# Joint rotation of two tiles, groups of three inner chunks, and an earlier start of the placing in a vision block with routed experts

## The chip, the cores and the metric

One core of a Trainium2 chip runs the whole program. The metric is device microseconds from launch to end; three runs of the kernel before were made, and one further execution was profiled. Times in the text are microseconds from the start of the span. The engines are called PE (TensorE), DVE (VectorE), ACT (ScalarE), POOL (GpSimd) and SP (SyncE, which only issues transfers).

## The reference

64 images of 224 x 224 become 196 patches each, 12544 rows of width 192 in all, and pass one block of a vision tower:

```
h = patches @ W + b
q, k, v = heads(layernorm(h))            # 12 heads of 16, q and k rotated by position
w = erf(q k^T / 4) + 1, causal; h = h + (w v / sum w) @ Wproj.T
x = layernorm(h)
probs = softmax(x @ Wr)                  # 8 experts, the best two per row, shares normed
each expert takes the 3920 rows that gave it the largest shares
expert(x) = (silu(x @ w1) * (x @ w3)) @ w2      # inner width 768
out = h + sum of chosen experts * share + shared expert(x)
```

All is float32. The rows chosen by an expert are scattered back with addition.

## The kernel before

**Attention** works in turns, one unit of two images (392 rows, four tiles) a turn, 32 units; turns overlap three stages, so that a turn computes the patch products of a later unit, norms and products q, k, v of the next one, the weights of its own, and the projection of the previous one. Each turn has twelve steps `n`, one per pair of heads. The order on every engine is written out by hand, as `if n == ...` lines. On DVE a step is multiply_x (L549), weigh (L556), a reciprocal (L608) and floor (L564), with other work between: at n == 3 and n == 4 the rotation of q and k, two tiles each (L626 to L633), at n == 5 the addition of the projection (L653), at n == 11 the bias (L663). The rotation takes the copy `qk_raw` that ACT made (L411 called from L445), multiplies it by a table of cosines and by one of sines, tile by tile (four instructions over 384 elements), waits, and forms differences and sums (four over 192). `settle` is a wait for all `step`s before. On ACT, at n == 3: a copy of scores (L420), the gelu (L435), two copies of the turned normed rows (`LN1T`, L439), then other copies. On PE, at n == 3: scores, weighted sums, the transposes of the normed rows (L734), twelve products of the second token tile (L748), which need the bank of the first `LN1T` copy, then q and k (L741), v, the turned outputs and at n == 5 the projection (L741 from L798). POOL multiplies the weights (L690) between ACT's gelu and DVE's weigh. Turn `u` is followed by the next without a gap.

**Routing.** `choices` forms for every row the two best experts and their shares, and then searches each expert's threshold, two bits a step (`search_and_place`, steps s = 0 to 15, s = 16 settles). Steps 0 to 10 run alone; the others, and the placing steps, run between chunks of the first five shared units, one step behind each pair of chunks (`behind_pair`, L1316). After the last count POOL sends the level to memory and back, spread over the experts (L1453, L1456). Step 17 is empty. Steps 18 to 23 rank the rows: two scans, each with a count on PE (`add_counts`, L1057), then `slots_of` for the first choices (s = 22) and for the second (s = 23), each of which raises `placed`. POOL waits for both, then scatters 196 entries into the table with indirect transfers (L1464), first and second choice of a row group in turn, never more than two in flight.

**Shared and expert units.** 25 shared units (512 rows, the last 256: SHORT) and 64 expert units (8 per expert, 490 rows) have one form. The inner width 768 is six chunks `m`. All products are in float16 parts, high and low. For a pair of chunks PE computes gate and up, per chunk eight whole-height matmuls (L1245 to L1248) and then, for both chunks, a half-height matmul for gate and one for up which run side by side (L1251, L1253). Behind each pair it issues a third of the output matmuls of the unit before (72 in all, L1274 to L1276). ACT forms the silu (L1290) and the high half of the hidden values (L1284), DVE the product (L1309) and the low half (L1302). Gate and up have two PSUM banks each; PE waits at a chunk until the chunk two before has been multiplied:

```
for m in (2 * pair, 2 * pair + 1):
    pe.wait_ge(T.multiplied, MI * g + m + 1)
```

The rows for an expert unit come by POOL's gather (L1476, four transfers by ids), are split into halves by ACT (L1576, L1577) and DVE (L1661, L1663), inside the unit before, behind chunk m == 1 (`split_at`; 3 in a whole shared unit), and SP issues four transposing transfers (L1428). Results are scaled by ACT (`put`, L1593) and scattered by POOL (L1487). Ahead of the first expert ACT and DVE split its weights behind the last whole shared unit (L1195, L1211).

## Time and profile before

| | |
|---|---|
| three runs | 3376.86, 3378.2, 3385.53 us, median 3378.2 |
| the profiled execution | 3376.83 us, span 3374.7 us |
| mean granted clock of PE | 0.945 of full speed |
| busy, share of the span | PE 3091.8 us (92%), DVE 2446.8 (73%), ACT 1526.7 (45%), POOL 1377.0 (41%) |
| instructions of the rotation | L626 and L627 x128 each over 384 elements, L631 and L633 x128 each over 192 |
| chunk work, mean of one | DVE L1309 670 ns, L1302 667 ns; ACT L1290 582 ns, L1284 601 ns |

Attention fills the span up to about 1600 us, the routing that runs alone up to about 1720, the shared units up to about 2200, and the experts the rest. In the timeline views a row has the start and the time taken of a merged run of like instructions; a number in brackets is the idle time of the engine ahead of it, with what ended it. The time between the starts of two instructions can be shorter than the first one takes.

### The profile page before, as it was taken

To read this page: it belongs to the slowest core of one execution; us is meant where nothing else is said; L and a number is where in the kernel's file an instruction comes from. 1 tells how busy PE (TensorE), PEld (TensorE's weight loads), DVE (VectorE), ACT (ScalarE), POOL (GpSimd) and SP (SyncE) were. 2 spreads that over 40 slices of the span, in tenths; PEclk is the share of its full clock that TensorE was granted. 3 is DMA by queue.
4 is the path that set the end of the run, shared out by engine and by line. 5 is a ranking of instruction groups with operands and counts; after the bars stand their busy time and mean duration, and the time that the engine had idled before them with its cause. 6 is when DMAs were issued, how large, how long until landed. Compare 5 with 4: busy or idle time off the path is not lost. (4 is left out here: it accounts for less than half of the span.)

```text
span 3374.7 us, 70939 instructions
## 1 busy us (share of the span) xinstructions
PE 3091.8 (92%) x25828; PEld 2110.6 (63%) x25828; DVE 2446.8 (73%) x4893; ACT 1526.7 (45%) x3223; POOL 1377.0 (41%) x1172
## 2 busy tenths in 40 slices
PE   6999999999999999998059999899999999999997
PEld 5777777777777777766025555556666556566664
DVE  6999999999999999997766555554555455455543
ACT  2444444444444444443024444444555455455443
POOL 1332233223332332322202555536666555655664
PEclk9899999999999999986579999999999999999999
DMA  3333333323332333322122222245554555545442
GB/s 104 77 75 78 73 87 80 81 66 87 89 76 68 81 89 75 75 46 54 45 67 67 74 67 78 59 95 101 77 96 71 98 71 97 101 69 97 77 75 42
DMA packets 460505, 260.36 MB, mean 77 GB/s; under 512 B 337967, under 2 KB 441759, under 8 KB 456063
## 3 DMA queue, kind: packets, MB, share of 16 engines
q1 hardware_dynamic: 392448, 196.41, 24.3%
q0 software_dynamic: 54464, 49.01, 10.3%
q10 hardware_dynamic: 13262, 10.66, 0.9%
q8 instruction: 192, 3.15, 0.4%
q14 instruction: 139, 1.14, 0.1%
HBM read 107.98 MB, written 68.15 MB: 52 GB/s over the span
## 5 line engine op out<-in xcount | busy, mean ns | idle before, releaser
L1309 DVE SCALAR_TENSOR_TENSOR ffn_hidden<-ffn_up,ffn_silu 128x490 f32<-128x490 f32 (+2 forms) x534 | 350.6, 670 | 676.2 <-ACT ffn_silu L1290 510.9
L690 POOL TENSOR_TENSOR weights<-weights,x_pair 128x400 f32<-128x400 f32 x384 | 396.3, 1032 | 828.7 <-DVE weights L556 810.1
L1290 ACT ACTIVATE ffn_silu<-ffn_gate 128x490 f32<-128x490 f32 (+2 forms) x534 | 301.9, 582 | 735.6 <-PE ffn_up L1253 541.6
L1487 POOL DMA_INDIRECT out_rows<-done,ids x256 | 407.4, 1591 | 407.6 <-ACT done L1593 346.4
L608 DVE RECIPROCAL recip<-x_product 128x200 f32<-128x200 f32 x384 | 534.2, 1391 | 0.0
L1274 PE MATMUL ffn_out<-ffn_w_hi,ffn_hidden_hi 128*128 128x192 f16 (+1 forms) x2124 | 525.6, 247 | 3.9 <-DVE ffn_hidden_lo L1302 2.0
L1275 PE MATMUL ffn_out<-ffn_w_lo,ffn_hidden_hi 128*128 128x192 f16 (+1 forms) x2124 | 522.8, 246 | 0.0
L1276 PE MATMUL ffn_out<-ffn_w_hi,ffn_hidden_lo 128*128 128x192 f16 (+1 forms) x2124 | 522.7, 246 | 0.0
L748 PE MATMUL bank<-w_tok,patches 128*128 128x192 f32 x1536 | 327.2, 370 | 56.8 <-ACT normed_t L411 32.7
L1302 DVE TENSOR_TENSOR ffn_hidden_lo<-ffn_hidden,ffn_hidden_hi 128x490 f16<-128x490 f32 (+2 forms) x534 | 356.3, 667 | 15.9
L1284 ACT CAST ffn_hidden_hi<-ffn_hidden 128x490 f16<-128x490 f32 (+2 forms) x534 | 320.7, 601 | 91.9 <-DVE ffn_hidden L1309 90.7
L748 PEld LDWEIGHTS bank<-w_tok,patches 128*128 128x128 f32 x1536 | 290.4, 217 | 72.8 <-ACT normed_t L411 39.2
L1476 POOL DMA_INDIRECT tokens<-dram_x,ids x256 | 279.1, 1090 | 91.1 <-issue 76.2
L420 ACT ACTIVATE x_pair<-score 128x400 f32<-128x400 f32 x384 | 192.5, 502 | 269.2 <-DVE weights L556 180.4
L857 PE MATMUL y_sum<-v_held,weights 128*64 128x68 f32 (+1 forms) x1536 | 262.4, 253 | 31.5 <-DVE weights L564 31.5
L1274 PEld LDWEIGHTS ffn_out<-ffn_w_hi,ffn_hidden_hi 128*128 128x128 f16 (+1 forms) x2124 | 219.2, 103 | 110.3 <-issue 98.5
L1464 POOL DMA_INDIRECT dram_table<-entry,slot_of x196 | 202.9, 1035 | 207.4 <-issue 131.8
L435 ACT ACTIVATE weights<-x_pair 128x400 f32<-128x400 f32 x384 | 205.0, 534 | 182.0 <-PE y_sum L863 177.5
L741 PE MATMUL bank<-w_qkv,normed_t 96*128 96x192 f32 (+1 forms) x1024 | 275.5, 418 | 0.7 <-ACT normed_t L411 0.7
L859 PE MATMUL y_sum<-v,weights 128*64 128x51 f32 (+2 forms) x1536 | 248.3, 244 | 0.0
L1245 PE MATMUL ffn_gate<-ffn_tokens,ffn_w_hi 128*128 128x490 f16 (+2 forms) x534 | 199.8, 374 | 36.3 <-DVE ffn_tokens L1230 12.4
L741 PEld LDWEIGHTS bank<-w_qkv,normed_t 96*128 96x128 f32 x1024 | 180.3, 192 | 68.9 <-issue 4.4
(176 smaller groups left out, 6862.2 us busy)
## 6 DMA issues: line engine op xcount, KB each, us to landing
patches<-in_patches SPq DMA_DIRECT2D x32, 1176.0 KB, 5.2
ffn_raw<-in_w SPq DMA_DIRECT2D x18, 768.0 KB
dram_x_t<-x_t SPq DMA_DIRECT2D x32, 392.0 KB, 3.7
x_t<-dram_x_t SPq DMA_DIRECT2D x24, 512.0 KB
base<-dram_h SPq DMA_DIRECT2D x24, 384.0 KB, 4.2
out_rows<-sums ACTq DMA_DIRECT2D x24, 384.0 KB, 4.6
v_held<-v SPq DMA_DIRECT2D x64, 102.0 KB, 2.3
dram_h<-h SPq DMA_DIRECT2D x32, 192.0 KB
```

Of the source, the lines that this page charges most:

```text
L608: nc.vector.reciprocal(recip[:, n % 2], x_product[:, n % 2]).then_inc(inverted, 1)
L690: nc.gpsimd.tensor_tensor(weights[:, n % 4], weights[:, n % 4], x_pair[:, n % 4, ::-1], ALU.mult)\
L741: last = nc.tensor.matmul(out, wide(lhs, k, t), rhs[:, k, 0:width], start=(k == 0), stop=(k == 1))
L748: last = nc.tensor.matmul(out, wide(patches[slot], i, n), tok_w[:, i, :], start=(i == 0), stop=(i == KP - 1))
L1274: nc.tensor.matmul(out, hi, w_hi[:, m, :], start=(m == 0), stop=False)
L1275: nc.tensor.matmul(out, hi, w_lo[:, m, :], start=False, stop=False)
L1276: last = nc.tensor.matmul(out, lo, w_hi[:, m, :], start=False, stop=(m == MI - 1))
L1284: nc.scalar.copy(T.hidden_hi[slot][:, m, 0:n], T.hidden[:, m % 2, 0:n]).then_inc(T.hi_ready, 1)
L1290: nc.scalar.activation(T.silu[:, m % 2, 0:n], T.gate[m % 2][:, 0:n], ACT.Silu, scale=1.0 / (TOKEN_SCALE * WEIGHT_SCALE)).then_inc(T.silued, 1)
L1302: nc.vector.tensor_tensor(T.hidden_lo[slot][:, m, 0:n], T.hidden[:, m % 2, 0:n], T.hidden_hi[slot][:, m, 0:n], ALU.subtract).then_inc(T.lo ...
L1309: nc.vector.scalar_tensor_tensor(T.hidden[:, m % 2, 0:n], T.up[m % 2][:, 0:n], HIDDEN_SCALE / (TOKEN_SCALE * WEIGHT_SCALE), T.silu[:, m % ...
L1487: nc.gpsimd.indirect_dma_start(out=dram["out"][:, :], out_offset=bass.IndirectOffsetOnAxis(ap=ids[i][0:height, t, 0:1], axis=0), in_=done[ ...
```

## The change

Four things change. In the attention the rotation handles two tiles in one instruction: two multiplications over 768 elements and two sums over 384 in place of four and four, after a wait for both tiles' copies; and ACT's two `LN1T` copies stand ahead of the gelu at n == 3. In the routing the placing steps begin at 17 rather than 18, and POOL scatters all first choices as soon as they have their slots, then all second choices. In the shared units from the sixth on and in all expert units chunks go in groups of three: three banks for gate and up (the third are the routing's two banks `total` and `offset`), a wait at a chunk for the one three before, the half-height matmuls of three chunks together, and half of the unit before's output matmuls behind each group; ACT and DVE index the banks by `m % group`. Between the fifth and the sixth shared unit PE waits for all multiplications. The split of the next rows stands ahead of the chunks in expert units, behind the last chunk in the SHORT unit, and behind chunk 2 in the others of groups of three. The last output part is issued as one.

```diff
-        by_cos = [sb(f"by_cos{s}", [128, 2 * NH, 2, HD // 2]) for s in range(2)]
-        by_sin = [sb(f"by_sin{s}", [128, 2 * NH, 2, HD // 2]) for s in range(2)]
+        by_cos = sb("by_cos", [128, 2, 2 * NH, 2, HD // 2])
+        by_sin = sb("by_sin", [128, 2, 2 * NH, 2, HD // 2])
...
+                    if n == 3 and has_next:
+                        for k, pos in enumerate(LN1T):
+                            copy_out(pos, normed_t[:, k * UT:(k + 1) * UT], KD)
...
-                    if n == 3 and has_next:
-                        for k, pos in enumerate(LN1T):
-                            copy_out(pos, normed_t[:, k * UT:(k + 1) * UT], KD)
...
                         for i in range(2):
-                            t = 2 * (n - 3) + i
-                            dve.wait_ge(free[QK[t] % NB], fills(kind, u, QK[t]))
-                            src = qk_raw[:, t, :].rearrange("p (h c f) -> p h c f", h=2 * NH, c=2)
-                            if i == 0:
-                                settle()
-                            step(nc.vector.tensor_tensor(by_cos[i][:], src, over(tables[:, i, 0, :], shape), ALU.mult))
-                            step(nc.vector.tensor_tensor(by_sin[i][:], src, over(tables[:, i, 1, :], shape), ALU.mult))
+                            dve.wait_ge(free[QK[t + i] % NB], fills(kind, u, QK[t + i]))
                         settle()
-                        for i in range(2):
-                            t = 2 * (n - 3) + i
-                            step(nc.vector.tensor_tensor(rotated[:, t, :, 0:HD // 2], by_cos[i][:, :, 0, :],
-                                                         by_sin[i][:, :, 1, :], ALU.subtract))
-                            step(nc.vector.tensor_tensor(rotated[:, t, :, HD // 2:HD], by_cos[i][:, :, 1, :],
-                                                         by_sin[i][:, :, 0, :], ALU.add))
+                        src = qk_raw[:, t:t + 2, :].rearrange("p i (g f) -> p i g f", f=HD // 2)
+                        for c, out in enumerate((by_cos, by_sin)):
+                            table = tables[:, :, c, :].unsqueeze(2).to_broadcast([128, 2, 4 * NH, HD // 2])
+                            step(nc.vector.tensor_tensor(out[:].rearrange("p i h c f -> p i (h c) f"), src, table, ALU.mult))
+                        settle()
+                        step(nc.vector.tensor_tensor(rotated[:, t:t + 2, :, 0:HD // 2], by_cos[:, :, :, 0, :],
+                                                     by_sin[:, :, :, 1, :], ALU.subtract))
+                        step(nc.vector.tensor_tensor(rotated[:, t:t + 2, :, HD // 2:HD], by_cos[:, :, :, 1, :],
+                                                     by_sin[:, :, :, 0, :], ALU.add))
...
-PLACING = SEARCHED + 2
+PLACING = SEARCHED + 1
...
+    T.gate.append(R.total)
+    T.up.append(R.offset)
...
+def units_group(g):
+    return 2 if isinstance(g, int) and g < ROUTING else 3
...
+def tensor_group(nc, pe, T, g, slot, ws, n, part, group):
+    chunks = range(group * part, group * part + group)
...
+        pe.wait_ge(T.multiplied, MI * g + m + 3 - group)
...
+def tensor_out(nc, pe, T, g, slot, ws, tiles, part, parts):
...
-    share = len(tiles) * MI // 3
-    for k in range(third * share, (third + 1) * share):
+    share = len(tiles) * MI // parts
+    for k in range(part * share, (part + 1) * share):
...
 def scalar_unit(nc, act, T, g, slot, n, split, split_at):
+    if split_at is None:
+        split()
...
-            pool.wait_ge(R.placed, 2)
-            pool.sem_inc(spacer, 1)
-            for n in range(2 * PER):
+            for n, (c, t) in enumerate((c, t) for c in range(2) for t in range(PER)):
+                at = 2 * t + c
+                if t == 0:
+                    pool.wait_ge(R.placed, c + 1)
+                    pool.sem_inc(spacer, 1)
                 if n >= 2:
 
                     pool.wait_ge(dispatched[n % 2], 16 * (n // 2))
                     pool.sem_inc(spacer, 1)
                 nc.gpsimd.indirect_dma_start(
                     out=dram["table"][:, :],
-                    out_offset=bass.IndirectOffsetOnAxis(ap=slot_of[:, n:n + 1], axis=0),
-                    in_=entry[:, 2 * n:2 * n + 2], in_offset=None, bounds_check=SLOTS - 1, oob_is_err=False)\
+                    out_offset=bass.IndirectOffsetOnAxis(ap=slot_of[:, at:at + 1], axis=0),
+                    in_=entry[:, 2 * at:2 * at + 2], in_offset=None, bounds_check=SLOTS - 1, oob_is_err=False)\
...
+                group = units_group(g)
+                for part in range(MI // group):
+                    tensor_group(nc, pe, T, g, slot, 0, columns_of(tiles), part, group)
                     if isinstance(g, int) and g < ROUTING:
                         add_counts(nc, pe, R, SERIAL + 3 * g + part)
                     if not (isinstance(g, int) and g == 0):
-                        tensor_out(nc, pe, T, g - 1, 1 - slot, 0, WHOLE, part)
+                        tensor_out(nc, pe, T, g - 1, 1 - slot, 0, WHOLE, part, MI // group)
+                if isinstance(g, int) and g == ROUTING - 1:
+                    pe.wait_ge(T.multiplied, MI * g + MI + 2)
+                    pe.wait_ge(R.placed, 2)
...
+                for part in range(2):
+                    tensor_group(nc, pe, T, g, 1 - i % 2, ws, XU, part, 3)
                     if opening(e, i):
-                        tensor_out(nc, pe, T, g - 1, 0, 0, SHORT, part)
+                        tensor_out(nc, pe, T, g - 1, 0, 0, SHORT, part, 2)
                     else:
-                        tensor_out(nc, pe, T, g - 1, i % 2, 1 - ws if i == 0 else ws, ROUTED, part)
+                        tensor_out(nc, pe, T, g - 1, i % 2, 1 - ws if i == 0 else ws, ROUTED, part, 2)
...
-            for part in range(3):
-                tensor_out(nc, pe, T, SHARED + XUNITS - 1, 0, 0, ROUTED, part)
+            tensor_out(nc, pe, T, SHARED + XUNITS - 1, 0, 0, ROUTED, 0, 1)
...
-                scalar_unit(nc, act, T, g, slot, columns_of(tiles), split_next, 1 if tiles is SHORT else 3)
+                scalar_unit(nc, act, T, g, slot, columns_of(tiles), split_next, MI - 1 if tiles is SHORT else 2 if units_group(g) == 3 else 3)
...
-                scalar_unit(nc, act, T, g, 1 - i % 2, XU, split_next, 1)
+                scalar_unit(nc, act, T, g, 1 - i % 2, XU, split_next, None)
...
```

DVE's `vector_unit` is changed as `scalar_unit` is.

## Rows read from the trace of the kernel before

**Rows 1.** Busy time by stretch; after the span PE, PEld, DVE, ACT, POOL, clock, DMA

```profile
917.16:964.27 47.11, 45.28 (x440) 35.07 (x440) 45.94 (x104) 22.83 (x53) 14.45 (x14) 0.96 0.31 80
964.27:1012.73 48.46, 45.32 (x440) 35.10 (x440) 46.19 (x104) 22.59 (x53) 14.46 (x14) 0.96 0.34 78
...
2210.00:3340.00 1130.00, 1122.20 (x8316) 676.84 (x8314) 577.55 (x921) 569.73 (x1153) 660.96 (x492) 1.00 0.49 85
```

**Rows 2.** DVE in order of time, the rotation at n == 3, turn A

```profile
931.62 0.55 DVE L626 TENSOR_TENSOR by_cos<-qk_raw,rope 128x384 f32<-128x384 f32 x1
932.09 0.55 DVE L627 TENSOR_TENSOR by_sin<-qk_raw,rope 128x384 f32<-128x384 f32 x1
...
933.61 0.36 DVE L631 TENSOR_TENSOR rotated<-by_cos,by_sin 128x192 f32<-128x192 f32 x1
933.89 0.35 DVE L633 TENSOR_TENSOR rotated<-by_cos,by_sin 128x192 f32<-128x192 f32 x1
...
935.00 0.37 DVE L549 SCALAR_TENSOR_TENSOR x_product<-x_pair 128x200 f32<-128x200 f32 x1 [0.23 <-DVE rotated L633]
```

**Rows 3.** ACT in order of time, n == 3, turn A

```profile
924.47 0.50 ACT L420 ACTIVATE x_pair<-score 128x400 f32<-128x400 f32 x1 [1.82 <-DVE weights L556]
924.87 0.53 ACT L435 ACTIVATE weights<-x_pair 128x400 f32<-128x400 f32 x1
925.30 0.85 ACT L411 COPY normed_t<-bank 96x392 f32<-96x392 f32 x2
```

**Rows 4.** PE in order of time, the same place in turns A and B

```profile
925.82 2.22 PE L748 MATMUL bank<-w_tok,patches 128*128 128x192 f32 x12 [1.17 <-ACT normed_t L411]
...
972.93 3.64 PE L748 MATMUL bank<-w_tok,patches 128*128 128x192 f32 x12 [1.25 <-ACT normed_t L411]
```

**Rows 5.** DVE in order of time, addition of the projection in turn B

```profile
990.81 0.56 DVE L653 TENSOR_TENSOR h<-bank,h 128x384 f32<-128x384 f32 x1 [0.46 <-PE bank L741]
992.01 0.56 DVE L653 TENSOR_TENSOR h<-bank,h 128x384 f32<-128x384 f32 x1 [0.64 <-PE bank L741]
```

**Rows 6.** PE in order of time, one pair of chunks in an expert unit

```profile
3102.88 0.37 PE L1245 MATMUL ffn_gate<-ffn_tokens,ffn_w_hi 128*128 128x490 f16 x1
...
3105.98 0.37 PE L1248 MATMUL ffn_up<-ffn_tokens,ffn_w_hi 128*128 128x490 f16 x1
3106.29 0.38 PE L1251 MATMUL ffn_gate<-ffn_tokens,ffn_w_lo 64*128 64x490 f16 x1
...
3106.81 0.26 PE L1274 MATMUL ffn_out<-ffn_w_hi,ffn_hidden_hi 128*128 128x192 f16 x1
...
3108.80 0.37 PE L1245 MATMUL ffn_gate<-ffn_tokens,ffn_w_hi 128*128 128x490 f16 x1
```

**Rows 7.** POOL in order of time, levels and first table scatter

```profile
1769.09 0.96 POOL L1456 DMA_DIRECT2D levels<-dram_level  x1 [4.28 <-DMA dram_level<-level]
1816.00 1.07 POOL L1464 DMA_INDIRECT dram_table<-entry,slot_of  x1 [45.95 <-issue]
```

**Rows 8.** The tile levels, how long its transfer took

```profile
DMA to landing us min/median/max: 5.0/5.0/5.0
```

**Rows 9.** DVE in order of time, the first placing step

```profile
1778.73 0.98 DVE L923 TENSOR_TENSOR scratch<-key,levels 128x784 f32<-128x784 f32 x1
...
1780.75 1.79 DVE L1076 TENSOR_TENSOR_SCAN running<-carry,key 128x784 f32<-128x784 f32 x1
```

**Rows 10.** PE in order of time, the count behind the first scan

```profile
1782.60 0.39 PE L1057 MATMUL offset<-running,before 128*128 128x8 f32 x2 [3.05 <-DVE running L1076]
```

**Rows 11.** PE in order of time, the short unit ahead of the experts

```profile
2182.88 0.39 PE L1245 MATMUL ffn_gate<-ffn_tokens,ffn_w_hi 128*128 128x256 f16 x1 [7.88 <-DVE ffn_hidden L1309]
...
2193.75 0.28 PE L1245 MATMUL ffn_gate<-ffn_tokens,ffn_w_hi 128*128 128x256 f16 x1 [4.36 <-issue]
```

**Rows 12.** ACT in order of time, the start of an expert unit

```profile
3080.34 1.35 ACT L1593 ACTIVATE done<-ffn_out,ids 128x192 f32<-128x192 f32 x4
```

**Rows 13.** POOL in order of time, the last gather for that unit

```profile
3077.03 1.00 POOL L1476 DMA_INDIRECT tokens<-dram_x,ids  x1 [0.30 <-issue]
```

39 lines of the change are left out of this document (19 added, 20 removed).

## The prediction

> **What bounds the kernel now.** I read the page's slices first: VectorE (DVE) is at nine tenths or more through the attention, nothing is full in the middle where the routing is worked out, and TensorE (PE) is full from the shared units to the end. Then busy time by stretch, in which the reader should see two things [rows 1]. Two neighbouring turns of the attention loop (one turn is one unit of two images), which I call A and B, last 47.11 and 48.46 us, with DVE busy for 45.94 and 46.19 us of them; and over 1130 us of experts PE is busy for 1122.20 us at full clock. The busy figure is short of the truth for DVE: instructions start before the one in front has ended (931.62, then 932.09, each 0.55 us long [rows 2]). So in turn A DVE is the bound. The 31 turns alternate between these two kinds in most of the stage.
>
> In order of time, B differs from A at one place. The 12 products of the second token tile take 2.22 us in A and 3.64 us in B, both behind a wait for ACT's copy of the turned normed rows, of 1.17 and 1.25 us [rows 4]. 3.64 us is what the half clock (1.2 GHz) makes of it for most of its length; the mean granted clock is 0.96 in both turns [rows 1], so A has such a drop too, elsewhere, where PE has time. All PE work from there to the projection is one string, so in B the projection is 1.42 us late, and DVE waits for it, 0.46 and 0.64 us [rows 5]. With the overlap lost at either wait (some 0.08 us each) that is nearly the whole 1.35 us by which B is longer. So B is bound by PE from that copy to the projection, A by DVE with next to nothing to spare (1.42 less 1.26: about 0.1 us).
>
> **Part 1, the joint rotation.** A multiplication over 384 elements starts 0.47 us ahead of the next, a sum over 192 elements 0.28 us [rows 2]. 192 elements more cost 0.19 to 0.20 us, so the fixed part is 0.07 to 0.09 us, and I take 0.07. The block from 931.62 to 935.00 is 3.38 us long; four of its eight instructions fall away and the elements stay: 4 x 0.07 = 0.27 us, or 0.54 us for the two blocks of a turn. New is a wait: the first multiplication needs both tiles copied. Queued behind it are the rotation and everything on DVE after it, and POOL, which waits for DVE's next weighting. In A both copies are in before DVE comes. In B the second multiplication pair of the first tile hides the second copy now; some 0.5 us of wait can appear there, but it takes its time from the wait at the projection, which comes later in the same turn, so I price it at nothing. As for the duration of an instruction rather than its distance: the Trainium skill (VectorE: DVE Perf Modes, "The TRN2 errata") puts a float32 tensor_tensor at (N+151)/0.96 ns, thus 0.157 us fixed. The trace's 0.55 us durations agree with it, its distances don't; by that fixed part the turn would lose 1.26 us rather than 0.54.
>
> **Part 2, the copies ahead of the gelu.** ACT runs the score copy at 924.47, the gelu at 924.87 and both copies from 925.30 [rows 3]. The copies move ahead of the gelu: 925.30 - 924.87 = 0.43 us earlier, and so does PE's string. The gelu comes 0.85 us later; POOL needs it only one DVE iteration of over 3 us after that, so this costs nothing. The PE transposes that the copies need are done before the score copy is.
>
> **What both make of a turn.** A: 47.11 - 0.54 = 46.57 us, for the projection comes 0.43 us earlier and there was 0.1 us of room. B: the saved DVE time only lengthens the wait; what counts is PE's 0.43 us, or half of it (0.21) where the half clock stays where it is in time, since then 0.43 us more of the products fall under it. So 48.46 becomes 48.03 to 48.25, and I take 48.14. Were the mix one to one, the gain would be 47.79 - 47.36 = 0.43 us a turn, 13 us over 31 turns. But the mix is what I trust least: where the drop falls hangs on where PE idles, and DVE's quicker side leaves PE the later one more often. Ends: only turns A, 31 x (47.79 - 46.57) = 38 us; only turns B, at 48.25, 31 x (48.25 - 47.79) = 14 us lost. I choose two B for one A, 47.62 us, a gain of 5 us, because the change makes PE's string the later one of the two and that is the condition of a turn B.
>
> **Part 3, the empty step and the scatters.** The placing step moves from the end of the second pair of the third shared unit to the end of the first. The levels' second transfer is issued at 1769.09 and takes 5.0 us [rows 7, 8], so they are there at 1774.1; DVE would come to the step some microseconds earlier, right behind that pair's first `lo`, and stand. The step takes 1782.54 - 1778.73 = 3.8 us [rows 9], thus until 1777.9. Queued behind it on DVE are the multiplications of that unit's other chunks; PE's count waits for its scan, and behind the count stand the output matmuls. PE ended the pair in front of its present wait at 1782.60 - 3.05 = 1779.5 [rows 10]. The pair before ended 6.1 us earlier (5.92 us [rows 6] with its whole matmuls lengthened by 512/490), at 1773.4. So PE waits some 4.7 us, to 1778.1, in place of 3.05: 1.6 us lost. Bounds: nothing (later stalls of the routing absorb it) and 5 us. The first scatter starts some 11 us before 1816.00 [rows 7], one step for the empty one and one for first choices first, less the loss. 196 scatters follow at POOL's pace to the end of the shared units, where today a PE wait of 4.36 us [rows 11] stands behind the last scatter, the ids and the gather. New there: PE waits once, after the fifth unit, for all multiplications, since the banks change their meaning. The last one is about 0.7 us behind PE: 0.7 us lost.
>
> **Part 4, groups of three.** A pair of an expert unit lasts 3108.80 - 3102.88 = 5.92 us [rows 6]. The 15 distances from its first to its last whole matmul are (3105.98 - 3102.88)/15 = 0.207 us; 24 output matmuls take 1.99 us (0.083 each). 18 x 0.207 + 1.99 = 5.71 us, so 0.21 us is the price of going from whole-height matmuls to half-height ones (0.31 instead of 0.21) and back (0.52 for two packed pairs instead of 0.41). A unit pays it twice rather than three times: 64 x 0.21 = 13.4 us for the experts, 20 x 0.21 = 4.2 us for the shared units from the sixth on. What must hold: DVE and ACT drain three chunks, on DVE 3 x (0.67 + 0.67) = 4 us by the means in the table above, while PE does the output part, 3.0 us, and the next group, 5.6 us. They do. Behind the wait for the next gather, now ahead of a unit's chunks on ACT and DVE, stand the silus: the put ends at 3081.69 [rows 12], the gather's last issue at 3078.03 [rows 13], 3.7 us before it, and the silus are not due for over 3 us more. Nothing, with 0 to 2 us gained where PE waits for the transposes today.
>
> At the short unit PE waits 7.88 us for the weights of the first expert, which DVE and ACT split, and then the 4.36 us [rows 11]. The second wait goes, since the split is moved behind the last chunk, but split and transposes then come later, and the weights are what is late: I take 0.7 us gained, between a loss of 3 and a gain of 4.
>
> **Sum**: 5 + 4.2 + 13.4 + 0.7 - 1.6 - 0.7 = 21 us. The profiled execution took 3376.83 us for a span of 3374.7, 1.4 us below the median of 3378.2; 3376.8 - 21 = 3355.8 by the profiled execution, 3357.2 by the median. Two or three waits for transposes that the earlier split may save bring it to 3355, my forecast for the median.
>
> **The rivals.**
> (a) Every turn is an A. For it: the gap at which PE idles is 0.43 us shorter. Against: a drop exists in both kinds today, and PE's idle time in a turn only shrinks by 0.5 us in some 3. 38 in place of 5: 3322 us.
> (b) Every turn is a B, 48.03 to 48.25 us: 8 to 14 us lost in place of 5 gained: 3369 to 3375 us. For it: parts 1 and 2 speed DVE more than PE.
> (c) Larger groups save nothing, as the half-height matmuls' price is per chunk and not per change. The rows speak against it, the second pair follows the first at 0.21 us. 17.6 us less gain: 3373 us. The Trainium skill (TensorE: Matmul & The Clock Gate, "Measured speedup vs the span model") gives packed tiles one matmul's time plus 4 ns and names no price for the change; by it the groups would bring nothing, against 0.21 us in the rows.
> (d) Slower: the gather wait at the head of the expert unit decides. If rows land later than about 3.7 + 3 us after the last issue, each unit's silus and, past the output part, PE slip. From 7 us on it costs 1 us a unit and more per us; 0.6 us a unit is already 38 us, which takes the gain and ends at 3394 us.
> (e) The change doesn't do what it says: the joint multiplication walks a broadcast table over two tiles and runs slower than 1 element a cycle. At 0.2 us per instruction more, four a turn, it eats the 0.54 us: in the range.
>
> **How the numbers follow.** Forecast 0.70 (3342 to 3364, by its unknowns: one to one or three to one of the turns, the levels 0 to 5, the short unit -3 to +4), (a) 0.13, (b) 0.09, (c) 0.04, (d) 0.04. A measurement of this kernel can tell some 0.3% from no change, 10 us: faster is below 3368. (b) and (c) count as same, with a little of the forecast's edge and against a little of (b)'s; (d) as slower: 0.83, 0.13, 0.04. The range reaches halfway to (a) and to the near end of (b): 3328 to 3369.
>
> **What would show it.** Two multiplications of about 0.95 us and two sums of 0.55 us per block, a block of 3.1 us. The copies of the normed rows straight behind a score copy, PE's wait there 0.75 us. Turns of 46.6 and 48.1 us, and how many of each. Expert units of 17.5 us (17.75 now). PE's count waiting some 4.7 us for the scan at the third shared unit, the first scatter near 1805. I would be wrong if turns of 47.8 us stood side by side without a drop, or if a wait of ACT for tokens ahead of the silus showed in the expert units.

## The result and the profile after

The changed kernel takes 3345.2 us, the median of four runs (3345.1 to 3350.1), beside 3378.1 us for the kernel before: a ratio of 0.9902, 95% interval 0.9885 to 0.9919, thus 33 us less. Forecast were 3355 us and a range of 3328 to 3369. In a later session the unaltered kernel came to 0.9909 (0.9894 to 0.9924). Single runs of one kernel differ by 3 to 20 us; what its profiles show of that is part of what follows.

The first view is busy time by stretch. The four stretches are the same in both kernels: from TensorE's (PE's) first matmul of the first shared unit through the five routing units, the other whole shared units, the short unit, and the experts up to the last unit's first matmul. After the span stand PE, PEld, DVE, ACT and POOL busy, each with its count, then the granted clock, the DMA share and GB/s. The kernel before:

```profile
1716.42:1823.41 106.99, 91.80 (x605) 50.60 (x606) 78.74 (x146) 42.83 (x75) 6.93 (x7) 0.97 0.19 59
1823.41:2170.23 346.82, 346.55 (x2511) 203.84 (x2510) 192.86 (x305) 157.70 (x286) 192.15 (x186) 1.00 0.24 72
2170.23:2200.21 29.98, 16.79 (x134) 12.38 (x133) 11.80 (x21) 8.59 (x16) 17.92 (x17) 0.77 0.30 73
2200.21:3327.59 1127.38, 1119.45 (x8280) 673.93 (x8281) 577.14 (x923) 568.52 (x1149) 655.84 (x489) 1.00 0.49 85
```

The changed kernel:

```profile
1705.60:1819.13 113.53, 94.06 (x604) 51.93 (x605) 79.88 (x147) 43.38 (x76) 13.92 (x13) 0.95 0.19 56
1819.13:2161.52 342.39, 342.39 (x2509) 207.00 (x2509) 191.56 (x303) 159.64 (x285) 189.72 (x185) 1.00 0.24 73
2161.52:2190.59 29.07, 13.96 (x134) 11.51 (x133) 15.35 (x29) 10.62 (x21) 15.12 (x14) 0.83 0.39 93
2190.59:3300.87 1110.28, 1105.12 (x8280) 684.36 (x8281) 573.92 (x914) 567.92 (x1144) 640.81 (x487) 1.00 0.50 86
```

Read the starts and the lengths. The attention and the choices end 10.8 us earlier (1716.42, 1705.60), the five routing units take 6.5 us more, the shared units 4.4 less, the short one 0.9 less, the experts 17.1 less; the rest of the span is equal within 0.2. That makes the 26.5 us between the two spans, 3374.7 and 3348.2. (The profiled execution of the changed kernel is its slowest of four, 3350.1 us, so the two spans differ by less than the medians.)

**The attention.** Five neighbouring turns of the changed kernel, busy time by stretch with the same columns:

```profile
963.82:1012.10 48.28, 45.57 (x440) 35.35 (x440) 45.59 (x96) 22.70 (x53) 14.45 (x14) 0.96 0.32 78
1012.10:1058.72 46.62, 45.38 (x440) 35.22 (x440) 45.45 (x96) 22.83 (x53) 14.45 (x14) 0.96 0.35 81
1058.72:1105.33 46.61, 43.89 (x440) 33.67 (x440) 45.44 (x96) 22.72 (x53) 14.44 (x14) 1.00 0.35 81
1105.33:1152.90 47.57, 46.67 (x440) 36.07 (x440) 45.66 (x97) 23.02 (x53) 14.43 (x14) 0.93 0.32 80
1152.90:1200.40 47.50, 46.70 (x440) 36.09 (x440) 45.68 (x96) 22.93 (x53) 14.44 (x14) 0.93 0.36 80
```

PE and DVE in order of time in the third of them (start, duration, engine, line, operation, then the idle time before it and what ended it):

```profile
1066.96 2.22 PE L746 MATMUL bank<-w_tok,patches 128*128 128x192 f32 x12 [0.83 <-ACT normed_t L411]
1073.18 0.95 DVE L627 TENSOR_TENSOR by_cos<-qk_raw,rope 128x768 f32<-128x768 f32 x1
1074.04 0.95 DVE L627 TENSOR_TENSOR by_sin<-qk_raw,rope 128x768 f32<-128x768 f32 x1
1075.03 0.56 DVE L629 TENSOR_TENSOR rotated<-by_cos,by_sin 128x384 f32<-128x384 f32 x1
1075.51 0.55 DVE L631 TENSOR_TENSOR rotated<-by_cos,by_sin 128x384 f32<-128x384 f32 x1
1076.29 0.37 DVE L549 SCALAR_TENSOR_TENSOR x_product<-x_pair 128x200 f32<-128x200 f32 x1 [0.23 <-DVE rotated L631]
1084.12 1.05 DVE L651 TENSOR_TENSOR h<-bank,h 128x384 f32<-128x384 f32 x2
```

The block of [rows 2] now takes 1076.29 - 1073.18 = 3.11 us, as forecast (3.38 before), and PE's wait for the normed rows is 0.83 us (forecast 0.75; 1.17 in [rows 4]). The last row is the addition of the projection: in this turn it waits for nothing. In the first of the five, which is of kind B, the second tile's 12 products take 3.90 us, DVE waits 0.78 us ahead of its first joint multiplication and 0.40 us for the projection (0.46 and 0.64 in [rows 5]). The strict change of A and B turns is gone. There are 46.6 and 48.3, and new kinds: 47.5 with more time at half clock (0.93, the 12 products of the first token tile take 4.21 us), 46.6 with none at all (1.00), and 49.

**The experts.** PE in order of time at the start of an expert unit of the changed kernel:

```profile
3090.55 0.37 PE L1255 MATMUL ffn_gate<-ffn_tokens,ffn_w_hi 128*128 128x490 f16 x1
...
3095.31 0.37 PE L1258 MATMUL offset<-ffn_tokens,ffn_w_hi 128*128 128x490 f16 x1
3095.61 0.38 PE L1261 MATMUL ffn_gate<-ffn_tokens,ffn_w_lo 64*128 64x490 f16 x1
```

23 distances from 3090.55 to 3095.31 are 0.207 us each, then 0.30 to the first half-height one, as in [rows 6]. An expert unit follows the one before it at 17.53 us (17.74 before), the median of 63.

**The routing.** PE's count behind the first scan, and DVE's placing step, in the changed kernel:

```profile
1763.99 0.98 DVE L921 TENSOR_TENSOR scratch<-key,levels 128x784 f32<-128x784 f32 x1 [4.63 <-DMA levels<-dram_level]
1766.00 1.79 DVE L1074 TENSOR_TENSOR_SCAN running<-carry,key 128x784 f32<-128x784 f32 x1
1767.85 0.60 PE L1055 MATMUL offset<-running,before 128*128 128x8 f32 x2 [4.97 <-DVE running L1074]
```

DVE stands 4.63 us for the levels and PE 4.97 us for the scan (3.05 in [rows 10]), close to the forecast 4.7. The third shared unit by stretch shows what else this costs. In the kernel before:

```profile
1763.20:1784.80 21.60, 18.55 (x137) 10.98 (x135) 13.88 (x21) 8.48 (x16) 1.82 (x2) 1.00 0.28 62
```

In the changed one:

```profile
1752.60:1777.65 25.05, 20.08 (x138) 12.34 (x136) 15.03 (x22) 8.22 (x15) 1.82 (x2) 0.93 0.26 53
```

1.9 us are the longer wait; another 1.5 us are PE's matmuls (20.08 for 18.55): the mean granted clock is 0.93 where it was 1.00, so part of them ran at the half level behind the longer wait. The first scatter is issued at 1798.1 us, 92.5 us behind the first shared unit; before it was 1816.0, 99.6 us behind it [rows 7]. That is 7 us earlier in the stage, where about 11 were forecast with the loss taken off.

### The profile page after: what moved, and what is told of

It reads as the page before. It is cut to its first block, busy times and chain, and to the rows that moved or that the text cites. A ratio compares the mean times of both kernels' runs of the same rounds, so it can differ in the third digit from the quotient of the medians.

```text
span 3348.2 us, 70681 instructions
## 1 busy us (share of the span) xinstructions
PE 3069.4 (92%) x25828; PEld 2122.7 (63%) x25828; DVE 2430.5 (73%) x4637; ACT 1532.7 (46%) x3223; POOL 1363.0 (41%) x1172
## 4 chain that ended last, share of the span: by engine, by line
PE 44%; DVE 2%; issue 2%; ACT 1%; DMA 1%; POOL 0%; ACTq 0%; DVEq 0%; SPq 0%; POOLq 0%
PE ffn_out L1284 5%; PE ffn_out L1285 5%; PE ffn_out L1286 5%; PE ffn_gate L1261 3%; PE ffn_gate L1255 2%; PE ffn_gate L1258 2%; PE ffn_up L1255 2%; PE ffn_gate L1257 2%; PE ffn_gate L1256 2%; PE ffn_up L1256 2%; PE ffn_up L1257 2%; PE ffn_up L1258 2%; PE total L1255 1%; PE offset L1257 1%; PE offset L1258 1%
## 5 line engine op out<-in xcount | busy, mean ns | idle before, releaser
L1329 DVE SCALAR_TENSOR_TENSOR ffn_hidden<-ffn_up,ffn_silu 128x490 f32<-128x490 f32 (+2 forms) x366 | 237.9, 670 | 562.1 <-ACT ffn_silu L1305 394.2
L1305 ACT ACTIVATE ffn_silu<-ffn_gate 128x490 f32<-128x490 f32 (+2 forms) x366 | 204.5, 584 | 672.2 <-PE ffn_up L1263 522.5
L1499 POOL DMA_INDIRECT tokens<-dram_x,ids x256 | 266.8, 1042 | 89.1 <-issue 80.1
L1285 PEld LDWEIGHTS ffn_out<-ffn_w_lo,ffn_hidden_hi 128*128 128x128 f16 (+1 forms) x2124 | 220.1, 104 | 0.1
```

The source lines that it names most:

```text
L1285: nc.tensor.matmul(out, hi, w_lo[:, m, :], start=False, stop=False)
L1499: nc.gpsimd.indirect_dma_start(out=rows[slot][0:height, t, :], out_offset=None, in_=dram["x2"][:, :], in_offset=bass.IndirectOffsetOnAxis( ...
```

## The experiments

Twelve kernels. For each I give the ratio to the kernel before in the same session, whose own median was 3379.0 to 3381.7 us, and what the profile shows, counted from the first shared unit, so that the attention's luck stays out.

**1. The attention's two edits alone**, in the kernel before:

```
-                            step(nc.vector.tensor_tensor(by_cos[i][:], src, over(tables[:, i, 0, :], shape), ALU.mult))
+                            step(nc.vector.tensor_tensor(out[:].rearrange("p i h c f -> p i (h c) f"), src, table, ALU.mult))
...
+                    if n == 3 and has_next:
+                        for k, pos in enumerate(LN1T):
```

> The kernel before with the joint rotation and the earlier copies of the normed rows, nothing else. Theory A (the attention gave more than the prediction's 5 us, because the last two turns, which rotate nothing, also came out shorter): TensorE's first matmul of the first shared unit comes some 11 us before the 1716.42 us of the kernel before, everything behind it keeps its distances, and the median falls by 8 to 12 us. Rival P (the prediction's term): the gain is 5 us, that is 5 us in 31 turns and nothing in the last two. Rival L (where the half clock falls moves with any change of times): profile and timed runs differ by several us and the share of turns of 46.6, 48.3 and 49.2 us differs from that of the changed kernel.

0.9951 (0.9937 to 0.9964), thus 16.5 us, the span of the profile 6.4 us shorter: it is the slowest of the six executions (3370.4 us, median 3365.9). The last two turns were not shorter there, so that half of theory A was a chance of one execution. The time lies in the turns that rotate, 1447.1 us from the first to the last bias addition for 1456.0, and the prediction's 5 us was too little. Rival L holds beside it: profile and timed runs differ by 8 to 10 us, and the mix of turns is another one than in the changed kernel. The 16.5 us themselves lie above theory A's 8 to 12.

**2. The joint rotation alone**, the first of these two hunks with its buffers:

```
+        by_cos = sb("by_cos", [128, 2, 2 * NH, 2, HD // 2])
```

> The kernel before with the joint rotation alone. Theory B (DVE bounds only one kind of turn): turns of kind A fall from 47.1 to 46.6 us, the others stay at 48.4 to 48.5 because DVE's gained time becomes a wait for the token product's string, and the mix moves towards the long ones: the first count matmul after the attention comes 0 to 5 us earlier than in the kernel before. The rotation block is 3.1 us long where it was 3.4. Rival M (the skill's fixed part of 0.157 us an instruction): a block 0.63 us shorter, 2.75 us. Rival Z (DVE bounds every turn): 0.54 x 31 = 17 us gained, ratio 0.995.

1.0006 (0.9995 to 1.0018): nothing. Two neighbouring turns by stretch:

```profile
917.57:964.60 47.03, 45.40 (x440) 35.23 (x440) 45.49 (x96) 22.67 (x52) 14.43 (x14) 0.96 0.32 81
964.60:1013.31 48.71, 45.57 (x440) 35.35 (x440) 45.60 (x97) 22.66 (x53) 14.42 (x14) 0.96 0.32 77
```

DVE in order of time, its waits in them for PE and ACT:

```profile
943.89 0.56 DVE L651 TENSOR_TENSOR h<-bank,h 128x384 f32<-128x384 f32 x1 [0.37 <-PE bank L739]
...
980.34 0.96 DVE L627 TENSOR_TENSOR by_cos<-qk_raw,rope 128x768 f32<-128x768 f32 x1 [1.20 <-issue]
```

DVE has 0.5 us less to do and waits for it: 0.37 us for the projection in A, which becomes 47.03, and 1.20 us in B for the second copied tile, which ACT ends at 980.25. B is 48.71 us, a little longer than before, so that the new wait isn't shown to be free. Theory B had the sign; that A would fall to 46.6 by itself was wrong. Rival M is out: the block from 932.03 to 935.13 is 3.10 us long, not 2.75. A had 0.1 us of room ahead of the projection, as the prediction had worked out, and no more.

**3. The earlier copies alone**, ahead of the gelu:

```
+                    if n == 3 and has_next:
+                        for k, pos in enumerate(LN1T):
+                            copy_out(pos, normed_t[:, k * UT:(k + 1) * UT], KD)
```

> The kernel before with the copies of the normed rows ahead of the fourth gelu alone. Theory B: turns A stay at 47.1 us, the others fall from 48.4 to 48.5 by 0.2 to 0.4 us, and TensorE's string, 0.43 us earlier, leaves more turns at A: 4 to 10 us gained before the first count matmul. Rival Z (DVE bounds every turn): nothing, within 3 us of the kernel before, which itself varies by that much between profiles. Rival G (the later gelu holds POOL and then DVE up): turns longer than 47.1 and 48.5.

0.9995 (0.9983 to 1.0007): nothing that can be told. Two neighbouring turns by stretch:

```profile
963.11:1010.24 47.13, 45.32 (x440) 35.13 (x440) 45.96 (x104) 22.80 (x53) 14.45 (x14) 0.96 0.35 80
1010.24:1058.55 48.31, 47.13 (x440) 37.03 (x440) 46.15 (x105) 22.72 (x52) 14.45 (x14) 0.93 0.34 78
```

PE's wait for the normed rows is 0.69 us (1.17 in [rows 4]), DVE's 45.96 us are nearly what they were (45.94), and A stays at 47.13. The mean granted clock is 0.937 to 0.943 in the twelve executions of this kernel, 0.942 to 0.948 in those of the kernel before: more of PE's work fell under the half level, which works against the edit. From the first to the last bias addition the turns take 1456.0 us before (1457.3 and 1456.0 in experiments 4 and 5, whose attention is that of before), 1455.8 with the rotation, 1453.1 with the copies (3 to 4 us less, under theory B's 4 to 10), and 1441.9 to 1450.1 in the nine profiles with both, on average 1445.6. So 0.7 and 3.4 us alone, each from one profile, and 10.9 together. The timed runs say the same: nothing and nothing alone, each within 4 us, and 16.5 together.

**4. Groups of three and the earlier split alone**, in the kernel before:

```
+    return 2 if isinstance(g, int) and g < ROUTING else 3
...
-                vector_unit(nc, dve, T, g, 1 - i % 2, XU, split_next, 1)
+                vector_unit(nc, dve, T, g, 1 - i % 2, XU, split_next, None)
```

> The kernel before with groups of three chunks in the shared units from the sixth on and in the experts, with the earlier split, and nothing of the routing's or the attention's edits. Theory S (the first expert unit waits for the 196 scatters, which follow the routing at POOL's own pace): the 20 shared units end 4.2 us earlier and the short unit's second wait gives it all back, the first expert unit starts within 1 us of 2200.2 us, and the gain comes from the experts alone, 64 x 0.21 = 13.4 us and some 3.5 us of removed waits: 17 us, a median near 3361. Rival P (the prediction, which adds 4.2 for the shared units and 0.7 for the short one): the first expert unit starts 4 us earlier, 21 us in all, 3357. Rival C (larger groups save nothing): expert units of 17.74 us as before.

0.9932 (0.9919 to 0.9946), 23 us, more than the 17 and 21 expected. The shared units take 342.8 us (346.8 before), yet the first expert unit starts at 2200.14 us, where it was (2200.21), 21.4 us behind the issue of the last scatter at 2178.8 (21.6 behind 2178.6 before), and the experts take 1111.9 us. That is theory S in absolute times, but the first shared unit began 3.0 us later by chance. Counted from it the first expert unit comes at 480.8 us (483.8 before) and the last scatter at 459.4 (462.1), so the scatters were quicker in this execution. The equal distance behind the last scatter speaks for theory S; experiment 8 decides it.

**5. The routing's two edits alone**, in the kernel before:

```
-PLACING = SEARCHED + 2
+PLACING = SEARCHED + 1
...
+            for n, (c, t) in enumerate((c, t) for c in range(2) for t in range(PER)):
```

> The kernel before with the placing step one pair earlier and the first choices scattered first, nothing else. Theory S: the third, fourth and fifth shared unit grow from 60.2 to some 65.5 us (TensorE waits near 5 us for the scan, the wait brings a stretch at half clock, and the next steps come late as well), the scatters end some 17 us earlier than 2178.6, the short unit's second wait of 4.36 us goes, and the first expert unit starts within 2 us of 2200.2: a median of 3377 to 3380. Rival P (the prediction): 1.6 us lost in the routing and nothing beyond, a short unit without its 4.36 us, a median near 3375. Rival N (earlier scatters bring nothing, since the weights' split is what is late): 3383 to 3385.

1.0009 (0.9998 to 1.0019): 3 us slower, at the edge of what can be told. Routing units 111.9 us (107.0), short unit 27.1 (30.0): what the earlier scatters save there does not pay for the placing. The shared units take 2.3 us more and the experts 2.7, which no run here explains, and the first expert unit starts 488.1 us behind the first shared one (483.8 before). Theory S had the third to fifth unit right (65.1 us), but the last scatter comes only 8.6 us earlier in the stage, not 17.

**6. The padding DMAs first on SP**, in the changed kernel:

```
+            for i in range(8):
+                sp.dma_start(ids[i][XR:XR16, 3, :], dram["pads"]).then_inc(pads_in, 16)
             shared_units(sp, unit)
...
-            for i in range(8):
-                sp.dma_start(ids[i][XR:XR16, 3, :], dram["pads"]).then_inc(pads_in, 16)
```

> The changed kernel with the eight small DMAs that fill the ids' padding rows moved on SP's queue from behind the last read of base rows to the front of the shared units. Theory Q (after the change SP's queue and no longer POOL's scatters holds the first ids back: last scatter issued at 2161.5 us, eight padding DMAs from 2165.2 to 2168.4, ids read at 2168.5): the ids are read some 3.3 us earlier, TensorE's wait of 8.56 us ahead of the first expert unit falls to about 5.3 us, and the median is 3.3 us below that of the changed kernel, near 3342. Rival W (ACT and DVE, which split the first expert's weights until 2174 us and then drain the short unit, are what the first rows wait for): the wait stays near 8.5 us and the median near 3345.

0.9908 (0.9893 to 0.9922): nothing. SP in order of time at the short unit of the changed kernel (SPq rows are DMA issues):

```profile
2165.17 3.24 SPq L1434 DMA_DIRECT2D ids<-in_pads  x8
2168.52 2.84 SPq L1430 DMA_DIRECT2D ids<-dram_table  x8
```

ACT there:

```profile
2180.85 0.63 ACT L1603 ACTIVATE split_rows<-tokens 128x512 f16<-128x512 f32 x1
```

SP with the padding first:

```profile
2163.59 4.31 SPq L1433 DMA_DIRECT2D ids<-dram_table  x8
```

ACT with the padding first:

```profile
2178.03 0.39 ACT L1305 ACTIVATE ffn_silu<-ffn_gate 128x256 f32<-128x256 f32 x1
...
2179.50 0.62 ACT L1604 ACTIVATE split_rows<-tokens 128x512 f16<-128x512 f32 x1
```

The ids are read 3.7 us behind the short unit's start instead of 7.0, but ACT's split of the rows comes 19.6 behind it instead of 19.3: on ACT it stands behind the silus of the short unit's second group. Rival W holds: PE's wait ahead of the first expert unit is 8.68 us (8.56 in the changed kernel).

**7. The changed kernel with the placing step late**, first choices still first, and **8. without both routing edits**. The diff of 7, and what 8 has besides:

```
-PLACING = SEARCHED + 1
+PLACING = SEARCHED + 2
...
-            for n, (c, t) in enumerate((c, t) for c in range(2) for t in range(PER)):
+            pool.wait_ge(R.placed, 2)
+            pool.sem_inc(spacer, 1)
+            for n in range(2 * PER):
```

> The changed kernel with the placing step where it was (two behind the search), first choices still scattered first. Theory S: TensorE's wait for the scan falls from 4.97 to about 3.05 us, no half clock behind it, and the third to fifth shared unit take near 61 us instead of 66.5: 5 us gained at that place. The first scatter comes 5 to 6 us later, the last is issued near 2167, and the first expert unit starts only 0 to 2 us earlier than in the changed kernel, counted from the first shared unit (485 us): the ratio to the kernel before is 0.989 to 0.991. Rival P (the short unit does not hang on the scatters any more): the 5 us stay, the first expert unit starts 480 us behind the first shared unit, a ratio of 0.9885 or below.

> The changed kernel without both routing edits: placing two steps behind the search, all scatters behind the second choice's slots. Theory S: third to fifth shared unit as in the kernel before (60 us, one more for the wait behind the fifth), the last scatter is issued 462 us behind the first shared unit as in the kernel before, and the first expert unit starts 481 to 485 us behind it: the routing part is worth between 0 and minus 4 us here, a ratio of 0.989 to 0.990. Rival P (the prediction's sum, by which the routing part costs 1.6 us in the routing and saves the second wait of the short unit): a first expert unit 3 us later than in the changed kernel, 488 us behind the first shared unit, ratio 0.991.

0.9902 (0.9887 to 0.9916) and 0.9902 (0.9887 to 0.9918), both what the changed kernel has. PE's wait at the end of the short unit in kernel 7 (the one inside the unit is 6.16 us):

```profile
2191.39 0.57 PE L1255 MATMUL ffn_gate<-ffn_tokens,ffn_w_hi 128*128 128x490 f16 x1 [8.33 <-issue]
```

In kernel 8 (5.58 us inside the unit):

```profile
2188.34 0.57 PE L1255 MATMUL ffn_gate<-ffn_tokens,ffn_w_hi 128*128 128x490 f16 x1 [13.45 <-issue]
```

With the placing late the routing units take 107.9 us instead of 113.5 and the first expert unit starts 479.8 us behind the first shared one (485.0 in the changed kernel): theory S expected the scatters to hold it at 483 to 485, rival P's 480 is what came. Without both edits the scatters do hold it: a wait of 13.45 us and 484.9, theory S. Nor does the first scatter come later in kernel 7, as was expected: it is issued 92.1 us behind the first shared unit (92.5 in the changed kernel, 99.4 in kernel 8), since DVE has the first choices' slots 91.0 us behind it in kernel 7 and 91.5 in the changed one. The longer routing units eat the whole step that the earlier placing wins, and the 7 us are those of first choices first. So of the routing part the order of the scatters is worth 5 us at this place and the earlier placing costs 5.7; in the timed runs neither shows beyond the interval of 5 us.

**9. The best of the parts**: late placing, padding first, and the split of the first expert's weights between the short unit's two groups,

```
     for m in range(MI):
+        if m == MI // 2 and halfway is not None:
+            halfway()
```

in `scalar_unit` and `vector_unit`, where `halfway` is what stood ahead of the short unit. Beside it **10. the changed kernel once more**, with no edit.

> The changed kernel with the placing step two behind the search again, the padding DMAs ahead of the shared units on SP, and the split of the first expert's weights between the short unit's two groups instead of ahead of them. Theory H (DVE and ACT split those weights while TensorE's second group of the short unit waits for its banks): TensorE's wait of 6.2 to 6.6 us inside the short unit falls below 1 us, the rows then bound its end, the first expert unit starts 477 to 480 us behind the first shared unit (485.0 in the changed kernel, 479.8 with the placing late), and from the first shared unit to the end it takes 1631 to 1636 us where the changed kernel takes 1642.6; ratio 0.986 to 0.989. Rival O (the order does not matter, the rows and weights need the same time of DVE and ACT): 480 to 483 us and a ratio of 0.989 to 0.990.

> The changed kernel once more, unaltered, beside the other kernels of this call. The ratio to the kernel before is 0.9885 to 0.992 as measured; the profile tells how far two executions of one kernel differ: the attention's end within 3 us (first shared unit at 1702 to 1709), the part from there to the end within 2 us of 1642.6 if the half clock falls at the same loop boundaries, some 1.7 us more or less for each boundary where it does not.

0.9910 (0.9897 to 0.9923) and 0.9909: no gain, so there is no version here that beats the changed kernel. Theory H had the mechanism: the wait inside the short unit is gone and the rows bound its end. But the other wait has grown by as much. PE in order of time:

```profile
2185.33 0.57 PE L1255 MATMUL ffn_gate<-ffn_tokens,ffn_w_hi 128*128 128x490 f16 x1 [16.25 <-DMA ffn_tokens<-split_rows]
```

The short unit takes 28.7 us (29.1), rival O's reading, though the first expert unit starts 483.4 us behind the first shared one, later than both expectations: the routing units take 112.3 us here and 107.9 in kernel 7, with the same routing, and the first and the third of them have a granted clock of 0.77 and 0.89 (0.93 and 1.00 there). From the first shared unit to the end it is 1642.1 us, not 1631 to 1636. The unaltered kernel stayed within what was expected: 3351.3 us of span, 1642.5 us from the first shared unit to the end (1642.6). There is no half clock at either loop boundary of the experts, 1.8 us less, and the routing units (114.2 us) and the short one (30.0) took that back.

**11. Half-height matmuls per chunk**, in the changed kernel: in groups of three each chunk's two half-height matmuls follow its eight whole ones at once, six changes a unit instead of two:

```
             nc.tensor.matmul(out, hi[:, beyond], far, start=False, stop=False)
-    for m in chunks:
+        if group == 3:
+            half_height(m)
```

`half_height(m)` issues the two matmuls of L1261 and L1263 of the changed kernel.

> The changed kernel with the half-height matmuls of a chunk right behind its whole-height ones in all groups of three, thus six changes and back per unit instead of two, with the same matmuls. Theory (a change and back costs TensorE 0.21 us): 4 x 0.21 = 0.84 us more per unit, expert units of 18.37 us where 17.53 were, 85 x 0.84 = 71 us in all, near 3416 to 3420. Rival C (the price is per chunk, so larger groups had nothing to save): expert units of 17.53 us and the same time.

1.0091 (1.0074 to 1.0109) against 0.9909 in that session: 62 us more. Expert units follow at 18.38 us (18.37 expected), shared ones at 18.87 (18.02). From the first shared unit to the end it is 64.1 us; the 71 expected left out that a slower PE waits less at the short unit (26.6 for 29.1 us) and the loop boundaries. PE in order of time:

```profile
3269.68 0.37 PE L1265 MATMUL ffn_up<-ffn_tokens,ffn_w_hi 128*128 128x490 f16 x1
...
3269.98 0.38 PE L1249 MATMUL ffn_gate<-ffn_tokens,ffn_w_lo 64*128 64x490 f16 x1
3270.29 0.38 PE L1262 MATMUL ffn_gate<-ffn_tokens,ffn_w_hi 128*128 128x490 f16 x1
```

**12. The next rows' split back inside the expert unit**, in the changed kernel:

```
-                vector_unit(nc, dve, T, g, 1 - i % 2, XU, split_next, None)
+                vector_unit(nc, dve, T, g, 1 - i % 2, XU, split_next, 1)
```

and the same on ACT.

> The changed kernel with the split of the next rows back behind the second chunk of an expert unit, where it was. Prediction's step (the earlier split saves two or three waits for transposes): the waits of 0.28, 0.77 and 0.65 us at the units after the second and third loop boundary come back, 1 to 3 us more. Rival (the split ahead of the chunks was needed with groups of three, since the third chunk drains later): a wait in every unit, units of 17.6 us or more, from 6 us on. Rival (no effect): within 1 us in the profile from the first expert unit to the end.

0.9944 (0.9929 to 0.9958) against 0.9909: 12 us lost, where the prediction's step gave 1 to 3. The experts take 1122.6 us for 1110.3. PE's waits from the second expert unit to the last in this kernel (us in total, times, the longest):

```profile
PE ffn_gate L1255 <- DMA ffn_tokens<-split_rows: 7.6, 12, 1.8
PE ffn_gate L1255 <- issue: 5.3, 2, 2.8
PE ffn_gate L1255 <- DVE ffn_hidden L1329: 2.1, 3, 0.7
```

The same in the changed kernel:

```profile
PE ffn_gate L1255 <- issue: 5.2, 2, 2.8
```

So 9.7 us are waits in fifteen units and most of the rest PE's matmuls, 1107.6 us busy for 1105.1. The second expectation had the size (from 6 us on) but not the place: fifteen units wait, not two or three and not all. How late the split is stands in the unit behind the first loop boundary. PE's first matmul and SP's first transposing transfer, in the kernel before:

```profile
2647.44 0.37 PE L1245 MATMUL ffn_gate<-ffn_tokens,ffn_w_hi 128*128 128x490 f16 x1
2655.56 5.23 SPq L1428 DMA_TRANSPOSE ffn_tokens<-split_rows  x4
```

In this kernel:

```profile
2637.73 0.37 PE L1255 MATMUL ffn_gate<-ffn_tokens,ffn_w_hi 128*128 128x490 f16 x1
2647.51 5.21 SPq L1448 DMA_TRANSPOSE ffn_tokens<-split_rows  x4
```

The transfers are issued 9.78 us into the unit instead of 8.12, each the median over the expert units too, and a unit is 0.21 us shorter; in the changed kernel the median of the units is 4.98.

## Why the prediction was right, and where it was short

The direction and the range stand. The forecast was 23 us less, a sum of 21 and some 2 for waits that the earlier split may save, and 33 were measured. In the profile two terms are off, and they partly cancel: the attention, 10.8 us for 5, and the routing, 6.5 lost for 2.3. That the total came as near as it did is in part luck. The three parts alone (experiments 1, 4 and 5) make 16.5 + 23 - 3 = 36.5 us in timed runs, and 33 lies within their uncertainty.

**Joint rotation and copies.** Block 3.11 us, turn A 46.6, turn B 48.3 (forecast 46.57 and 48.03 to 48.25). The wait for both copied tiles shows in B, 0.78 us for some 0.5; that it costs nothing isn't shown. The failed step is the one the prediction trusted least, "I choose two B for one A": of the 30 full turns 12 are of the 46.6 kind and 9 of the 48.3 kind, the others of the new ones, and the mean is 47.48 us for 47.77 before, 0.29 a turn instead of 0.17. The term was 5 us; the nine profiles give 10.9, and experiment 1 gives 16.5 in time, with some 5 us of uncertainty. Experiments 2 and 3 settle the mechanism for A: DVE and PE's string were within 0.1 us of each other, so either edit alone leaves A at 47.0 and 47.1 us and only both bring it to 46.6. The prediction had this condition in its working for A, and it should have led it to call the two edits one. Why the mix of turns comes out as it does, no run shows. The further 4.6 us that the two traces differ by from the last bias addition to the shared units (226.4 and 221.8 us) are chance: of the other eight profiles with both edits five have 226.7 to 227.5, the changed kernel's own second one (227.2) among them.

**The fixed part of a DVE instruction.** 768 elements take 0.95 us and follow at 0.86 to 0.87; 384 follow at 0.47 to 0.48. Against the distances of before (0.47 for 384) the elements cost 0.40 and the fixed part is 0.07, as taken. Joining saved 0.27 us a block (3.38 to 3.11), as forecast, though 4 x 0.07 is 0.28. The 151 cycles of the Trainium skill (VectorE: DVE Perf Modes, "The TRN2 errata") fit the duration, (768 + 151)/0.96 = 957 ns, and not the distance: by them a block would have lost 0.63 us.

**The empty step.** The wait was sized rightly (4.97 for 4.7), its price was not: 6.5 us in the five routing units for a forecast 2.3 with the change of banks (0.84 for 0.7). Left out were the half clock behind the longer wait, 1.5 us, and the steps behind it, all late by then: PE waits 0.74, 0.49 and 1.58 us in the fourth and fifth unit, where before it waited 1.46 once. What the step was to bring, scatters one step earlier, didn't come either: experiment 7, with the step late, has the first scatter at the same place and gets 5.7 us back in the profile.

**The short unit.** 0.9 us for 0.7, but that is luck: the step behind it failed. PE's waits in the changed kernel, where the prediction had the second one go (7.88 and 4.36 us in [rows 11]):

```profile
2174.36 0.39 PE L1255 MATMUL ffn_gate<-ffn_tokens,ffn_w_hi 128*128 128x256 f16 x1 [6.55 <-DVE ffn_hidden L1329]
2190.59 0.57 PE L1255 MATMUL ffn_gate<-ffn_tokens,ffn_w_hi 128*128 128x490 f16 x1 [8.56 <-issue]
```

The two are 2.9 us longer together, and what made up for it is PE's own time, 13.96 us for 16.79, at a granted clock of 0.83 for 0.77. Experiments 6 to 9 show three ends of nearly one length: the weights' split, the scatters with the ids, and ACT's order in front of the rows' split. With the ids eased (6), or the ids and the weights' split (9), the unit still takes 29.5 and 28.7 us. With all scatters behind both choices (8) it takes 34.7: that also holds back what the shared units gain.

**Groups of three.** 0.21 us a change: 17.53 us a unit (17.5), 4.4 us in the shared units (4.2). Experiment 11 puts the price beyond doubt and ends rival (c): 18.38 - 17.53 = 0.85 us for four changes more. The pair of half-height matmuls does start together, at 3095.61; it is the way there (0.30 us instead of 0.207) and the way back (0.31 in experiment 11) that cost 0.1 us each. The Trainium skill's 4 ns for packed tiles (TensorE: Matmul & The Clock Gate, "Measured speedup vs the span model") says nothing of that way, and rival (c) had no more than this behind it.

**The earlier split** was priced at "nothing, with 0 to 2 us gained". It was the condition of the groups: without it the experts take 1122.6 us, 4.8 less than before, not 17.1. In a pair the first half-height matmul, which ends the first chunk, comes 3106.29 - 3102.88 = 3.41 us behind the start [rows 6], in a group of three 3095.61 - 3090.55 = 5.06. A split behind the second chunk slides back with it: the transposing transfers are issued 1.66 us later in experiment 12 (9.78 for 8.12), in a shorter unit, and PE waits at the start of fifteen units instead of three. Why at these and not at all, no run shows.

**Luck in the experts.** Of the 17.1 us 63 x 0.21 = 13.2 are the groups' and 2.0 the three waits that are gone. The remaining 1.9 us stand at one of two loop boundaries. By stretch in the kernel before:

```profile
2589.33:2647.44 58.11, 54.96 (x400) 32.58 (x398) 25.77 (x43) 25.90 (x54) 32.83 (x24) 0.97 0.45 86
2879.12:2936.65 57.53, 55.07 (x399) 32.65 (x398) 25.77 (x43) 25.90 (x54) 32.84 (x24) 0.97 0.45 86
```

In the changed kernel:

```profile
2575.00:2632.27 57.27, 54.43 (x398) 33.13 (x397) 25.78 (x42) 26.07 (x55) 31.73 (x24) 0.97 0.56 107
2860.22:2915.29 55.07, 52.75 (x399) 32.67 (x398) 25.77 (x42) 26.06 (x55) 31.64 (x24) 1.00 0.53 103
```

PE waits there for 2.3 to 3.2 us in all four, and the half clock follows in three of them. In experiment 10, the same kernel, it follows in none.

**Rivals.** (a) and (b), one kind of turn only, didn't come; (c) fell with experiment 11; (d) shows nowhere, no wait of PE's in the expert units but at the two boundaries; (e) didn't come either: 768 elements take 0.86 us to the next instruction, 384 took 0.47.

## What to carry to other kernels

Where two engines end a stretch within a tenth of a microsecond of each other, cost the two edits as one: here they gave 0.7 and 3.4 us alone (one profile each) and 10.9 together. When work is regrouped, look for what hangs on the moment of a step inside the group (here the split behind the second chunk): moving it along was worth 12 us beside the 13 that the groups save in the experts. And price a longer wait of TensorE with the half clock that can follow it and with the steps queued behind it, not by its length.

## What the runs showed of the hardware

The half clock follows a wait of PE in one execution and not in the next of the same program: of the two loop boundaries one has it in the first profile of the changed kernel and none in the second (experiment 10); in the kernel before both have it. It costs 1.7 to 1.9 us each time. The third shared unit with its wait of 3.05 us took 21.6 us at full clock in six of the eight profiles with the late placing, and 23.6 at 0.89 in two; with the early placing and a wait of 4.4 to 5.0 us the clock was 0.87 to 0.93 in all six. At such places, and in the mix of turns, profiles of like kernels differ by several us; that they make the whole spread of the timed runs isn't shown. A difference of 5 us between two kernels is better read from stretches of the trace than from the times, if more than one profile has it. Changing between whole-height and half-height matmuls cost 0.1 us each way, with one, two or three pairs of half-height ones between.
